# Half-block decay tables and a new slot order in a linear-bias attention stage (two adaLN layers)

## The reference, cut to what matters

```python
std_logits = jnp.einsum('bhqd,bhkd->bhqk', q, k) * scale
incidence = jnp.einsum('bqhp,bkhp->bhqk', read_lines, J_write)
weights = decays[:, None, None] ** diffs_pos[None] * past[None]
bias = incidence * weights[None] * bias_scale[None, :, None, None]
logits = jnp.where(causal_mask[None, None], -jnp.inf, std_logits + bias)
attn = jax.nn.softmax(logits, axis=-1)
out = jnp.einsum('bhqk,bhkd->bqhd', attn, v)
```

## Time and profile before

| | |
|---|---|
| median of 3 runs | 1305.91 us (1302.59 to 1307.32) |
| the profiled execution | 1308.25 us |
| its span, first to last instruction | 1307.0 us |
| mean granted clock of TensorE over the span | 0.857 |
| busy: PE, DVE, ACT, POOL | 70%, 66%, 39%, 29% |
| attention1's loop, first to last weigh (L1402) | 492.0 to 1046.5 us |

### The profile page before, as it was taken

The page is one execution under the profiler, slowest core; times in us unless marked ns, Lnnn a source line. Parts: engine busy times, 40 slices in busy tenths (PEclk is TensorE's granted clock), DMA queues, the critical chain, the costliest instruction groups (busy, mean ns, idle before and its releaser), DMA issues.

```text
span 1307.0 us, 22919 instructions
## 1 busy us (share of the span) xinstructions
PE 919.2 (70%) x8847; PEld 625.2 (48%) x8847; DVE 868.8 (66%) x1863; ACT 511.9 (39%) x930; POOL 373.1 (29%) x620
## 2 busy tenths in 40 slices
PE   3777825556560345788888888888888870789888
PEld 1444413444440224666666666666766750344444
DVE  4545447898967215778786868777788834666664
ACT  2333312213213220435344443444343442578666
POOL 0122122444421445252425334262521001010110
PEclk7889976767675555899999998999999995799999
DMA  3000000000000141233323142322332202000000
GB/s 105 1 1 0 1 17 0 1 0 1 1 1 18 44 112 32 67 87 85 87 55 101 39 127 45 93 66 76 87 86 45 46 2 89 1 17 1 17 17 17
DMA packets 49814, 55.16 MB, mean 42 GB/s; under 512 B 11180, under 2 KB 43404, under 8 KB 49704
## 3 DMA queue, kind: packets, MB, share of 16 engines
q1 hardware_dynamic: 48264, 52.33, 15.1%
q10 hardware_dynamic: 1440, 1.33, 0.4%
HBM read 29.30 MB, written 23.82 MB: 41 GB/s over the span
## 4 chain that ended last, share of the span: by engine, by line
PE 33%; issue 16%; DVE 15%; POOL 11%; ACT 7%; DMA 3%; SPq 1%; POOLq 0%; ACTq 0%; DVEq 0%
PE bank L1728 10%; DMA KA<-scr_a 3%; PE bank L1323 2%; PE bank L689 2%; PE bank L1277 2%; PE bank L690 2%; PE bank L1269 2%; POOL M L1208 2%; POOL M L1209 1%; PE bank L1284 1%; PE bank L1300 1%; PE bank L1270 1%; PE bank L1263 1%; PE bank L1290 1%; DVE mo L1418 1%
## 5 line engine op out<-in xcount | busy, mean ns | idle before, releaser
L1412 DVE TENSOR_REDUCE mo<-bank 128x4 f32<-128x512 f32 x128 | 88.7, 693 | 69.2 <-PE bank L1270 63.7
L1507 ACT ACTIVATE ET<-bank 128x512 f32<-128x512 f32 x128 | 76.7, 599 | 139.1 <-PE bank L1291 139.1
L1402 DVE TENSOR_TENSOR bank<-bank,W 128x512 f32<-128x512 f32 x128 | 88.6, 692 | 39.4 <-PE bank L1263 38.9
L1407 DVE TENSOR_TENSOR bank<-bank,WT 128x512 f32<-128x512 f32 x128 | 88.9, 694 | 37.7 <-PE bank L1284 36.6
L1728 PE MATMUL bank<-act,h 128*128 128x512 f16 x512 | 112.1, 379 | 0.1
L1269 PE MATMUL bank<-KB,QO 128*128 128x128 f16 x512 | 76.8, 230 | 42.1 <-DVE bank L1402 41.8
L1830 DVE TENSOR_TENSOR act<-4f,act 128x512 f16<-128x512 f32 x96 | 66.4, 691 | 55.6 <-ACT act L1783 55.3
L1503 ACT ACTIVATE ET<-bank 128x768 f32<-128x768 f32 x128 | 102.7, 802 | 1.0 <-PE bank L1300 0.2
L1300 PE MATMUL bank<-QO,KA 128*128 128x128 f16 x768 | 66.8, 225 | 37.0 <-ACT ET L1503 36.4
L1323 PE MATMUL bank<-ET,vv 128*32 128x128 f32 (+2 forms) x1792 | 90.7, 329 | 2.9 <-DVE O L1435 1.7
L1418 DVE TENSOR_REDUCE mo<-bank 128x4 f32<-128x512 f32 x128 | 87.0, 680 | 0.0
(11 more groups left out here) (292 smaller groups left out, 2232.9 us busy)
## 6 DMA issues: line engine op xcount, KB each, us to landing
QO<-scr_q SPq DMA_DIRECT2D x32, 252.0 KB
KA<-scr_a SPq DMA_DIRECT2D x32, 252.0 KB
KB<-scr_k SPq DMA_DIRECT2D x32, 96.0 KB
scr_a<-dk SPq DMA_DIRECT2D x8, 288.0 KB, 4.4
KC<-scr_k SPq DMA_DIRECT2D x32, 72.0 KB
X<-in_x SPq DMA_DIRECT2D x8, 256.0 KB, 6.8
scr_q<-std SPq DMA_DIRECT2D x8, 256.0 KB, 4.1
scr_k<-std SPq DMA_DIRECT2D x8, 256.0 KB, 4.1
```

Of the source, the lines that this page charges most:

```text
L1402: dve.tensor_tensor(tiles(psD), tiles(psD), over(W[:, h * P:(h + 1) * P], NT), ALU.mult).then_inc(s_wq, 1)
L1407: dve.tensor_tensor(tiles(psDT), tiles(psDT), over(WT[:, h * P:(h + 1) * P], NT), ALU.mult).then_inc(s_wk, 1)
L1412: dve.tensor_reduce(tiles(mo[g % 2][:, x * NT * NT:(x + 1) * NT * NT])[:, :, 0], tiles(psD), AX.X, ALU.max).then_inc(s_ra, 1)
```

## The change

The tables W and WT now cover only pairs of tokens within a half block of 64 (64 columns instead of 128). Between the two halves of a diagonal block the bias comes from decayed operands, which are new rows (R_NEAR = 18) of the query and key operands: the near keys dkn of the first halves and the near queries dqn of the second halves, made next to dk and dq on DVE, ACT and POOL and written by six more DMAs per sequence in runs of 64 fp16 numbers. So on_diagonal and its twin by key become two matmuls per block with outputs on 64 rows each, and one mask matmul for all four blocks; the incidences become two 64x64 matmuls per block. The weighings cover half the columns. The exp on the diagonal becomes two instructions. ET has 8 buffers instead of 7 and their never written quarter is cleared once. The tables are made with 2 large exps instead of 32 small ones. AHEAD goes from 10 to 11, the rows of values, turn_out and normalise come one round later, and each engine's order within a round is new.

```diff
-        R_STD, R_DEC, R_LINES = 3 * DH, 3 * DH + 3 * NL, 3 * DH + 6 * NL
+        R_NEAR = 3 * NL
+        R_STD, R_DEC, R_LINES = R_NEAR + 3 * DH, R_NEAR + 3 * DH + 3 * NL, R_NEAR + 3 * DH + 6 * NL
...
-        W, WT = sb("W", H * P), sb("WT", H * P)
+        W, WT = sb("W", H * HB), sb("WT", H * HB)
...
-        AHEAD = 10
+        AHEAD = 11
...
+                for n, x, z, parts in (("k", dkn, 0, (0, 1, 0)), ("q", dqn, 1, (0, 0, 1))):
+                    for i, hilo in enumerate(parts):
+                        sp.dma_start(half(blocks(n, p, NL * i, NL * (i + 1)), z), tiles(part(x, hilo, T // 2))).then_inc(s_wline, 16)
...
-                set_maxima(g)
                 if g + 2 < GROUPS_:
                     fetch(g + 2)
+                set_maxima(g)
...
+                    v = dve.tensor_tensor(tiles(dkn32), half(ps, 0), over(Dk[:, KX // 2 - HB:], NT), ALU.mult)
...
+                    v = dve.tensor_tensor(tiles(dqn32), half(ps, 1), over(Dq[:, 0:HB], NT), ALU.mult)
...
+                act.activation(part(dkn if j == 0 else dqn, 0, T // 2), dkn32 if j == 0 else dqn32, ACT.Copy).then_inc(s_d16, 1)
...
+                pool.tensor_tensor(part(near, 1, T // 2), near32, part(near, 0, T // 2), ALU.subtract).then_inc(s_dlo, 1)
...
             def incidences(n):
                 for a in range(NT):
-                    m = pe.matmul(psD[:, a * P:(a + 1) * P], block(QO, n, a), block(KC, n, a), start=a == 0, stop=False, skip_group_check=True)
+                    for z in HALVES:
+                        m = pe.matmul(psD[z, a * P + HB:(a + 1) * P], block(QO, n, a)[:, z], block(KC, n, a)[:, z], start=a == 0, stop=False, skip_group_check=True)
...
             def on_diagonal(n):
                 pe.wait_ge(s_wq, n + 1)
                 for a in range(NT):
-                    pe.matmul(psD[:, a * P:(a + 1) * P], block(QO, n, a), block(KB, n, a), start=False, stop=False, skip_group_check=True)
-                    m = pe.matmul(psD[:, a * P:(a + 1) * P], sh.identh, sh.maskh, start=False, stop=True, skip_group_check=True)
-                m.then_inc(s_own, 1)
+                    q, k = block(QO, n, a), block(KB, n, a)
+                    pe.matmul(psD[HB:P, a * P:(a + 1) * P], q[:, HB:P], k, start=False, stop=False, skip_group_check=True)
+                    pe.matmul(psD[0:HB, a * P + HB:(a + 1) * P], q[:, 0:HB], k[:, 0:HB], start=False, stop=False, skip_group_check=True)
+                pe.matmul(tiles(psD), sh.identh, over(maskq, NT), start=False, stop=True, skip_group_check=True).then_inc(s_own, 1)
...
-                dve.tensor_tensor(tiles(psD), tiles(psD), over(W[:, h * P:(h + 1) * P], NT), ALU.mult).then_inc(s_wq, 1)
+                dve.tensor_tensor(half(psD, 1), half(psD, 1), over(W[:, h * HB:(h + 1) * HB], NT), ALU.mult).then_inc(s_wq, 1)
...
-                act.activation(ET[n % NE][:, 0:T], psDT, ACT.Exp).then_inc(s_expd, 1)
+                act.activation(to[0:HB, :], psDT[0:HB, :], ACT.Exp)
+                act.activation(half(to[HB:P, :], 1), half(psDT[HB:P, :], 0), ACT.Exp).then_inc(s_expd, 1)
...
             for i, w in enumerate((W, WT)):
-                for h in range(H):
-                    a_ = act.activation(w[:, h * P:(h + 1) * P], D0[i], ACT.Exp, scale=lg[:, h:h + 1])
+                act.activation(w, w, ACT.Exp).then_inc(s_W, 1)
```

More of the change, by code:

```diff
@@ L910, in attention1 @@
         dq, dk = sb("dq", 2 * T, dt=F16, rows=NR), sb("dk", 2 * KX, dt=F16, rows=NR)
-        vv = [sb(f"vv{i}", NT * H * VH + 32) for i in range(3)]
+        dqn, dkn = sb("dqn", T, dt=F16, rows=NR), sb("dkn", T, dt=F16, rows=NR)
+        vv = [sb(f"vv{i}", NT * H * VH + 32) for i in range(NV)]
         M, L, sq, cp = sb("M", 8 * 2 * NR), sb("L", 8 * NR), sb("sq", 8 * NR), sb("cp", NT * NP4)
@@ L945, in attention1 @@
         hnow = lambda i: hT[:, 1 + i * P:1 + (i + 1) * P]
+        half = lambda x, i: tiles(x)[:, :, i * HB:(i + 1) * HB]
+        HALVES = (slice(0, HB), slice(HB, P))
         def place(n):
@@ L1283, in incidences_by_key @@
                 for a in range(NT):
-                    m = pe.matmul(psDT[:, a * P:(a + 1) * P], block(KC, n, a), block(QO, n, a), start=a == 0, stop=False, skip_group_check=True)
+                    for z in HALVES:
+                        m = pe.matmul(psDT[z, a * P:a * P + HB], block(KC, n, a)[:, z], block(QO, n, a)[:, z], start=a == 0, stop=False, skip_group_check=True)
                 m.then_inc(s_incT, 1)
@@ L1396, in on_pe @@
                 side(n)
+                if 0 <= j < HEADS:
+                    incidences_by_key(j)
+                if n < HEADS:
+                    below(n)
+                if n + 1 < HEADS:
+                    incidences(n + 1)
+                if 0 <= j < HEADS:
+                    on_diagonal_by_key(j)
+                if 0 <= j + 1 < HEADS:
+                    below_by_key(j + 1)
+                g, x = divmod(n - 5, G)
+                if x == 0 and 0 <= g < GROUPS_:
+                    turn_maxima(g)
         def on_dve():
@@ L1461, in on_dve @@
             for x in vv:
-                v = dve.memset(x, 1.0)
+                dve.memset(x, 1.0)
+            for x in ET:
+                v = dve.memset(half(x[HB:P, 0:T], 0), 0.0)
             v.then_inc(s_edge, 1)
+            dve.wait_ge(s_ln, 1)
+            dve.wait_ge(s_clamp, 1)
+            for w, d in zip((W, WT), D0h):
+                dve.tensor_tensor(tiles(w, H), over(d, H), each(lg, HB), ALU.mult).then_inc(s_arg, 1)
             dve.wait_ge(s_edge, 1)
@@ L1589, in on_pool @@
             for n in range(LAST):
-                if n and n % G == 0 and n // G - 1 < GROUPS_:
-                    maxima(n // G - 1)
                 b, x = divmod(n, H)
@@ L1596, in on_pool @@
                 side(n)
+                if n and n % G == 0 and n // G - 1 < GROUPS_:
+                    maxima(n // G - 1)
                 b = rows_at(n, 2)
```

139 lines of the change are left out of this document (77 added, 62 removed).

## The result

The changed kernel takes **1366.67 us**, the median of 4 runs (1360.75 to 1369.99), against 1305.39 for the kernel before (4 runs): 1.0465 times, 95% interval 1.0442 to 1.0489. It is slower by 61 us; the forecast was slower by 28, at 1334.

The account below looks back on a forecast made before the run. PE-ACT-PE chains, DVE and POOL take turns bounding attention1's slots. Five full sequences +25, the first +2, sixth and last together +1: +28 us, 1334 against the median 1305.91; range 1277 to 1372.

Parts of the forecast that it names:

- 1.4 us in each of four phases, some 45 us in all: Sign to look for: PE's first turn_out matmul waits this long for ACT's oS in phases 0, 4, 8 and 12.
- The walk by phase: Attention1's slot (one head's loop round) lengths, booked for each phase (n mod 16): 77.3 us per sequence against 72.3 before.
- DVE's gain: Both weighings shrink from 512 to 256 columns: 0.26 us saved twice per slot, counting only where DVE ends the slot.
- rival D: Short DMAs of the near operands delay the next sequence's fetch; seven sequences lose 28 us: 1362, chance 0.10.
- The lower clock: PE at 1.2 of 2.4 GHz behind phase 0's idle time: 0.7 us added to phase 1, an estimate.
- Phase 0: Slot whose length POOL's chain from cp through sq to DVE's n and weighing sets: 7.5 us.
- The first sequence: Sequence 0: early slots shorter, wait for POOL hides one slot less, later slots longer: +2 us.
- R: PE's tail in every slot, incidences, on-diagonal by key and below-diagonal by key issued in a row: 1.95 us.
- The wait of PE for DVE's weighing should nearly go: Sign to look for in PE's waits; the forecast gave it no size in us.
- A: Rival: narrow matmuls are cheap, width changes cost nothing, pairs cost their columns; 70 us per sequence, 1276, chance 0.18.
- B: Rival: pairs of narrow matmuls do not overlap, 0.44 instead of 0.22 us in four blocks; 1395, chance 0.10.
- C: Rival: no change, since the gaps fall into existing waits or half of each is hidden; 1306, chance 0.12.

Follow-up runs that it names:

- gather_early: Changed kernel with ACT's copy of the finished outputs (gather) taken one slot earlier, right behind the side steps: 1327.9 us, 1.0136 of the kernel before.
- full_tables: Kernel before with its whole tables and contents, seven exp buffers, and a new order with earlier gather, later PE side steps and sums of squares: 1247.5 us, 0.9533.

## Why the prediction was right in direction and half the size

**What held.** The mechanism is the one forecast: turn_out waits for an oS that ACT copies behind its exps. "1.4 us in each of four phases, some 45 us in all" was 54.8 us over 32 groups, 1.7 each. gather_early took it away and 43 us with it. The walk by phase held in 13 of 16 phases within 0.5 us, on the mean of the five full sequences; for sequence 3, with the forecast in brackets: phase 1 4.84 (4.5), 2 2.97 (3.4), 4 4.89 (4.8), 5 5.76 (5.6), 6 3.74 (3.8), 7 4.17 (4.2), 9 5.38 (5.3), 10 5.16 (5.0), 13 5.12 (5.35), 15 3.78 (3.8). DVE's gain was as booked, 0.26 per weighing, and rival D never showed: 0.2 us of waits for a fetch.

**The step that failed** is the sum's size, in four terms that were too small.

- *The lower clock, booked once, in phase 1.* It came behind the longest waits for oS as well. Over the five full sequences phase 8 took 7.3 on average (booked 6.2) and phase 12 7.1 (6.0): 2.1 us per sequence, 10.7 in five. In phase 8 turn_out starts 3.99 us behind the weighing in every sequence, and in phase 4, where the clock stays up, 2.06 us follow it: 6.05 at the full clock, near what was booked. Phase 12 separates the two best, for the wait is the same 1.89 us each time (PE's timeline of the changed kernel, sequences 1 and 4):

```profile
633.39 0.66 PE L1361 MATMUL bank<-ident,oS 128*128 128x128 f32 x4 [1.89 <-ACT oS L1570]
...
871.93 1.12 PE L1361 MATMUL bank<-ident,oS 128*128 128x128 f32 x4 [1.89 <-ACT oS L1570]
```

  In sequence 1 the clock stayed at full speed and the slot took 6.04 us, as forecast; in sequence 4 it was at half speed for six, and the slot took 8.07. Busy time by microsecond of the changed kernel in either:

```profile
634.00:635.00 1.00, 1.00 (x9) 0.84 (x7) 0.00 (x0) 0.00 (x0) 0.00 (x0) 1.00 0.40 49
635.00:636.00 1.00, 1.00 (x27) 0.79 (x28) 0.43 (x1) 0.00 (x0) 0.00 (x0) 1.00 0.66 176
...
872.00:873.00 1.00, 1.00 (x6) 1.00 (x6) 0.00 (x0) 0.00 (x0) 0.00 (x0) 0.50 0.52 123
...
877.00:878.00 1.00, 1.00 (x10) 0.74 (x11) 0.96 (x4) 0.57 (x1) 0.00 (x0) 0.50 0.02 6
```
  No run changed the clock by itself.
- *Phase 0, booked at 7.5.* It took 8.2 on average, 3.4 us more in five sequences, and there the clock had no part: it was 1.00 throughout in four of the five. POOL's chain sets the length: from the start of the last copy to cp to DVE's n<-sq it takes 10.8 us in each, booked at 10.9. But cp is ready some 0.2 later in its slot than booked, and phases 14 and 15, which run beside the chain, take 7.0 and not 7.2 (6.4 ahead of sequence 1, whose phase 0 takes 8.62). With phases 8 and 12 this is 2.8 us per sequence, all that the beat of 80.15 has over 77.3.
- *The end of the stage, booked at nothing.* It grew by 8.0 us, from 36.3 to 44.3. The last four groups wait for oS there too (6.5 us), and the values and all that follows come a slot later. In gather_early the end is 38.5 us long, so 5.8 of the 8.0 are that wait; 2.2 are left for the later slot.
- *The first sequence, booked at +2.* It took 6.2 more: its side steps from phase 8 on meet ACT's exps as in any other sequence (phases 8 to 10: 5.76, 6.86 and 6.42, before 4.63, 3.48 and 3.31), and I had let it off with a guess. Part of it seems to be the clock again: it is up from 0.50 to 1.00 at 531.5 us in the kernel before, in phase 8, and at 540.6 in the changed one, in phase 10. In the later sequences, mostly at 1.00, phases 9 and 10 take 5.4 and 5.2, 2.7 us less than here.

These are 14.2 (phases 8, 12 and 0) + 8.0 + 4.2 = 26.4. The last two sequences, the setup and ffn1 came out 0.4, 1.2 and 0.3 under what was booked, which leaves 24.5: the 52.5 of the traces less the 28 forecast. The 9 us between the traces' difference and that of the medians are the spread of the runs.

Terms were wrong and cancelled. The earlier fetches, which I had put at nothing, took away waits of PE for KA of 8.2 us in the last two sequences, and these still came out 0.6 longer: so what else changed there cost about as much. R, PE's tail, was booked at 1.95 us and is 1.73 (778.44 to 780.17): eight narrow incidences cost 0.16, not 0.22, between narrow neighbours, and the mask by key has 256 columns, where I counted 0.21 for 512. ACT's second exp, booked at 0.27 by its columns, takes 0.41 (767.43 to 767.84), and the first 0.60, not 0.49. Freed at 1.5 in place of 1.35, ACT answers 0.15 later, and the tail is 0.22 shorter.

**What would have shown it wrong.** "The wait of PE for DVE's weighing should nearly go" was wrong: 46.3 us now, 41.8 before. Most of it never was the weighing's length, but n<-sq standing in front of it, which waits for POOL (24.3 of the 41.8, and 24.0 of the 46.3). I had read the earlier trace rows so, and should have drawn that from it.

**The rivals.** A, cheap narrow products, was to decide from an R below about 1.6; R is 1.73. Its premise was partly true (the incidences are cheap), but not that a change of width costs nothing. B fell with the overlap of the pairs, 0.08 apart or less (779.28, then four pairs and the gap in 0.35). C wanted the gaps hidden in other waits; widening the products gave 12 to 33 us back, so they were not all hidden. The Trainium skill, "TensorEngine Tiling (Array Packing)", Key Properties, says that a change of tiling mode drains the array; the gaps of 0.1 at each crossing agree with it.

## What to carry to other kernels

When a change moves the consumer of a copy to an earlier place, move the producer too, or list for each of its waits which instructions the other engine issues first: one line in ACT's loop was worth 43 us here. A wait in front of the rest of a slot costs more than its length, if the clock falls meanwhile: book the work behind every such wait (1.4 us and more here) at both clock levels, not behind one of them. And a change that trades one engine's time for another's should be tried apart from the reordering: here half blocks lose 17 us even in the best order (1270.2 against 1253.0), and all of the 4.7% in full_tables comes from the order of the work, that of the fetches included.

## What the runs showed that was not expected

- Two exps that read PSUM on 64 partitions each, back to back, hold ACT for 0.60 and 0.40 us for 512 and 256 columns; one of 512 on 128 partitions holds it 0.49 to 0.50. Splitting one into two cost 0.5 us each time, 13 to 27 us per kernel.
- A wait of PE of 2.78 us was followed by a clock of 0.50 in all five full sequences, in four of them from before its end, in one from 1.1 us behind it. One of 1.89 us was followed by 0.50 in three and by 1.00 in two, and one of 1.40 (phase 4) by 0.50 in one of five, where its slot took 6.22 us and not 4.89, with the same instructions before it.
- The stage's mean clock is a poor guide: 0.89 in the changed kernel and 0.88 in gather_early, which is 39 us faster. What counts is which work lies in the stretches at half speed.
- Narrow incidences are faster than wide ones (0.16 against 0.24) only where the next block has the same width.
